# A two-pass rescaling kernel: the last stretch moved in 1 MB pieces in place of 2 MB ones

## What is computed

```python
x = x + _L0_conv_ref(_gn(x), w1, w2, g1, b1, g2, b2, lw1, lb1, lw2, lb2)
# _gn(v):        ((g - mean) / sqrt(var + eps)) in 32 groups
# _L0_conv_ref:  num = softmax(linear(linear(dot_cb)), axis=1);  return x * num[:, :, None, None]
```

## Time and profile before

| | us |
|---|---|
| median of 3 runs | 1735.64 |
| lowest, highest | 1733.91, 1736.18 |
| the profiled execution | 1736.04 |
| its span in the trace | 1734.3 |
| last stretch, from the first scaling of batch 1 to the end of the span | 587.9 |

### The profile page before, as it was taken

One profiled execution on the slowest core, in us unless ns is written; L12 is line 12 of the kernel. 1 busy time (PEld: TensorE's weight loads), 2 busy tenths in 40 slices (PEclk: granted clock), 3 DMA queues, 4 the chain that ended last, 5 costly groups with the idle time before them and its releaser, 6 DMA issues.

```text
span 1734.3 us, 12474 instructions
## 1 busy us (share of the span) xinstructions
PE 473.8 (27%) x3186; PEld 155.4 (9%) x3186; DVE 936.0 (54%) x4043; ACT 649.2 (37%) x504; POOL 327.8 (19%) x432
## 2 busy tenths in 40 slices
PE   3588756532223233233232332510000000000000
PEld 1233212110000010001000010100000000000000
DVE  5899999934655666555765557862222222222220
ACT  4688887853534545435454445400000000000000
POOL 7678888820000000000000000000000000000000
PEclk8799988866566665665666666755555555555555
DMA  9999999979999999999999998999999999999999
GB/s 390 426 426 426 404 413 426 428 295 425 425 432 429 429 431 429 431 431 429 430 431 429 430 425 348 372 384 433 429 430 433 430 431 433 430 431 433 430 431 394
DMA packets 52281, 725.97 MB, mean 419 GB/s; under 512 B 6257, under 2 KB 6769, under 8 KB 8050
## 3 DMA queue, kind: packets, MB, share of 16 engines
q1 hardware_dynamic: 34066, 460.94, 62.7%
q10 hardware_dynamic: 18144, 264.25, 35.8%
HBM read 456.73 MB, written 268.44 MB: 418 GB/s over the span
## 4 chain that ended last, share of the span: by engine, by line
DMA 54%; another core or an unknown queue 26%; DVE 6%; PE 4%; ACT 4%; issue 1%; SPq 1%; POOL 1%; ACTq 0%; POOLq 0%; DVEq 0%
DMA xs<-in_x 42%; DMA out<-xs 10%; DVE mul_junk L843 4%; PE ps_part L493 2%; ACT sq_junk L663 2%; DVE xs L920 2%; ACT xs L724 2%; DMA z<-in_w 1%; SPq L313 1%; PE ps_l L586 0%; PE ps_l L574 0%; SPq L260 0%; PE ps_y L594 0%; POOL rstd_b L401 0%
## 5 line engine op out<-in xcount | busy, mean ns | idle before, releaser
L843 DVE SCALAR_TENSOR_TENSOR mul_junk<-xs,ps_w 128x256 fp8e5<-128x256 f32 x1856 | 642.3, 415 | 275.0 <-DMA xs<-in_x 246.5
L663 ACT ACTIVATE sq_junk<-xs 128x4096 fp8e5<-128x4096 f32 x128 | 463.2, 3619 | 383.3 <-DMA xs<-in_x 363.2
L493 PE MATMUL ps_part<-xs,taps 128*32 128x512 f32 x2048 | 330.0, 800 | 619.7 <-DMA xs<-in_x 619.7
L920 DVE TENSOR_SCALAR xs<-xs,scale,shift 128x4096 f32<-128x4096 f32 x98 | 243.1, 2501 | 402.0 <-DMA xs<-in_x 401.4
L493 PEld LDWEIGHTS ps_part<-xs,taps 128*32 128x32 f32 x2048 | 88.5, 141 | 834.6 <-issue 815.3
L843 DVE DVE_READ_ACCUMULATOR mul_junk<-xs,ps_w 128x1 f32 x1856 | 151.2, 81 | 0.0
L401 POOL TENSOR_TENSOR rstd_b<-var,minus_half 128x2 f32<-128x2 f32 (+1 forms) x16 | 12.5, 778 | 689.3 <-DVE var L870 689.3
L373 POOL TENSOR_TENSOR prod<-xs,w_copy 128x768 f32<-128x768 f32 x64 | 116.6, 1828 | 60.3 <-DMA xs<-in_x 57.6
L724 ACT ACTIVATE xs<-xs,shift,scale 128x4096 f32<-128x4096 f32 x30 | 113.7, 3789 | 11.1 <-DVE xs L920 5.7
L379 POOL TENSOR_TENSOR prod<-prod 128x384 f32<-128x384 f32 x64 | 63.2, 1011 | 0.0
L383 POOL TENSOR_TENSOR prod<-prod 128x192 f32<-128x192 f32 x64 | 36.8, 600 | 0.0
(11 more groups left out here) (101 smaller groups left out, 280.6 us busy)
## 6 DMA issues: line engine op xcount, KB each, us to landing
xs<-in_x SPq DMA_DIRECT2D x215, 2048.0 KB, 25.0
out<-xs ACTq DMA_DIRECT2D x126, 2048.0 KB, 27.0
xs<-in_lw SPq DMA_DIRECT2D x2, 2048.0 KB, 21.3
out<-xs SPq DMA_DIRECT2D x2, 2048.0 KB, 11.0
w_c<-in_w_rows SPq DMA_DIRECT2D x1, 512.0 KB, 4.3
w_sb<-in_w SPq DMA_DIRECT2D x1, 512.0 KB, 9.5
z<-in_w SPq DMA_DIRECT2D x1, 512.0 KB, 23.6
affine_in<-in_g SPq DMA_DIRECT2D x2, 16.0 KB
```

Source lines behind the costliest of these rows:

```text
L493: last = nc.tensor.matmul(ps_part[g % 2][32 * a:32 * a + 32, :], taps[:, g % 2, hf * JH + j, :], xs[:, s[0]:s[1] + 1:s[1] - s[0], j * W:(j ...
L663: nc.scalar.activation(sq_junk[:], xs[:, s, :], ACT.Square, accum_out=sq_sum[:, u % 2, u // 2, b:b + 1], saturate=False).then_inc(squared, 1)
L843: last = nc.vector.scalar_tensor_tensor(out=mul_junk[:, sets[0] % 2, j - first, :], in0=xs[:, s, j * W:(j + 1) * W], scalar=1.0, saturate= ...
L920: return nc.vector.tensor_scalar(xs[:, s, :], xs[:, s, :], scale[:, b, g:g + 1], shift[:, b, g:g + 1], ALU.mult, ALU.add)
```

## The change

`CUTS` = 2 and `CUT` = `HALF // CUTS` (2048 elements) are new, and each half-unit of the last stretch is moved in two pieces of 128 x 2048, 1 MB, 8 KB in each partition. Each slot gets four semaphores of its own for it: `last_loaded[s][c]` and `last_stored[s][c]` for `c` = 0, 1; the last stretch no longer uses `x_loaded` and `x_stored`, except that loads 5 to 8 still wait for the batch 0 stores. SP issues 118 loads in place of 59, VectorE 128 scalings in place of 64, ScalarE's queue 128 stores in place of 64. A piece's load waits for the store of the same piece, nine half-units earlier. Nothing ahead of the last stretch is changed.

```diff
+CUTS = 2
+CUT = HALF // CUTS
+HELD_IN = (5, 4, 8, 6, 7)
...
-for _i in range(UNITS):
-    if _i >= HELD:
-        LOADS[last_slot(_i)].append(("last", _i))
-    STORES[last_slot(_i)].append(("last", _i))
...
+        last_loaded = [[sem(f"last_loaded{s}_{c}") for c in range(CUTS)] for s in range(S)]
+        last_stored = [[sem(f"last_stored{s}_{c}") for c in range(CUTS)] for s in range(S)]
...
+        def cut(u, c):
+            return slice((u % 2) * HALF + c * CUT, (u % 2) * HALF + (c + 1) * CUT)
...
             for i in range(HELD, UNITS):
                 s, u = last_slot(i), LAST_ORDER[i]
-                if i < S:
-                    sp.wait_ge(x_stored[s], written(s, ("x", UNITS - S + i, 0)))
-                else:
-                    sp.wait_ge(x_stored[s], written(s, ("last", i - S)))
-                sp.dma_start(xs[:, s, :], x_v[u // 2, :, 1, part_of(u)]).then_inc(x_loaded[s], 16)
+                for c in range(CUTS):
+                    if i < S:
+                        sp.wait_ge(x_stored[s], written(s, ("x", UNITS - S + i, 0)))
+                    else:
+                        sp.wait_ge(last_stored[s][c], 16 * (i // S))
+                    sp.dma_start(xs[:, s, cut(0, c)], x_v[u // 2, :, 1, cut(u, c)]).then_inc(last_loaded[s][c], 16)
             for s in range(S):
                 sp.wait_ge(x_stored[s], 16 * len(STORES[s]))
+                items = [i for i in range(UNITS) if last_slot(i) == s]
+                for c in range(CUTS):
+                    sp.wait_ge(last_stored[s][c], 16 * len(items))
...
             for i, u in enumerate(LAST_ORDER):
-                act.wait_ge(scaled_last, i + 1)
-                store(u, 1, last_slot(i))
+                s = last_slot(i)
+                for c in range(CUTS):
+                    act.wait_ge(scaled_last, CUTS * i + c + 1)
+                    act.dma_start(out_v[u // 2, :, 1, cut(u, c)], xs[:, s, cut(0, c)]).then_inc(last_stored[s][c], 16)
...
             for i, u in enumerate(LAST_ORDER):
                 s = last_slot(i)
-                if i >= HELD:
-                    dve.wait_ge(x_loaded[s], landed(s, ("last", i)))
-                scaled_by_dve(s, 1, u // 2).then_inc(scaled_last, 1)
+                g = u // 2
+                for c in range(CUTS):
+                    if i >= HELD:
+                        dve.wait_ge(last_loaded[s][c], 16 * (i // S if last_slot(i) in HELD_IN else i // S + 1))
+                    nc.vector.tensor_scalar(xs[:, s, cut(0, c)], xs[:, s, cut(0, c)], scale[:, 1, g:g + 1],
+                                            shift[:, 1, g:g + 1], ALU.mult, ALU.add).then_inc(scaled_last, 1)
```

## The result

The changed kernel takes 1741.16 us (median of 8 runs, 1739.4 to 1744.55), the kernel before 1736.3 us (8 runs beside them). The ratio on record is 1.0031 (the two medians alone give 1.0028), with a 95% interval of 1.0022 to 1.0040, or 3.8 to 6.9 us more. The forecast was 1741.4 us in a range of 1737.0 to 1749.0, with slower as the likely side.

A forecast was written before the change was run, and what follows sets the result against it. The prediction took the DMA engines' own time (bytes plus a cost per packet) to bound the last stretch. 1736.04 + 5.5 (packets) + 0.3 (last waits) + 0 = 1741.8, set to 1741.4 us against the median; range 1737.0 to 1749.0.

The forecast's parts named there:

- What bounds the stretch: Last stretch: the DMA engines' own time sets the period, 9.73 us per half-unit at 431 GB/s, not load or store delays.
- The packet term, 5.5 us: Last stretch: 1107 more packets on each engine at 5 ns beside their bytes, 5.5 us more.
- The 2 KB rows: Packet price from 2 KB loads set against 16 KB loads beside all engines' work: 6.6 ns per packet, 7.4 us.
- The 8 KB rows: Upper bound on packet price from a short window of 8 KB loads: 0.6 us per MB, 9.7 us over the stretch.
- The costless edits: Last stretch: VectorE's halved scalings and the added load and store issues fit inside existing waits and cost nothing.
- The 0.3 us for the last waits: Kernel's end: SP's 18 more waits, bounded by 0 and two issues of 0.33 us, taken as 0.3 us.
- Start and end, 0 us: Both ends of the last stretch: earlier first store and last scaling win nothing, 0 us; gain bounded by 1.2 + 1.5 us.
- The rival of a full queue: Last stretch: 14 queued stores block issues, perhaps holding up loads, 5 to 10 us beside the 5.5; with costs above 10, 0.08.
- A fixed cost for each DMA: Last stretch: rival named together with the full queue; the prediction said the trace disagrees as long as queues are deep.
- A cost in the loads or the stores alone: Last stretch: named as a sign that would make the forecast fall; no size given.
- The free pieces: Last stretch: smaller packets cost nothing and GB/s stays at 431; chance 0.11.
- the finer exchange: Last stretch: load and store packets alternate twice as often, 431 up to 437 GB/s, gain 8.1 us, 1727.6; chance 0.06.

The follow-up runs named there:

- e3: The change with four pieces in place of two (512 KB, 4 KB rows), against the kernel before: ratio 1.0090, +15.6 us.
- e1: Kernel before with 8 KB rows (alternate quarters of the group's row), still 2 MB DMAs; against the kernel before: ratio 1.0011, +1.9 us.
- e2: Kernel before with 1 MB DMAs split by odd and even partitions, still 16 KB rows; against the kernel before: ratio 1.0016, +2.8 us.
- e4: Kernel before with only VectorE's scalings in halves, loads and stores still 2 MB; against the kernel before: ratio 0.9997, -0.5 us.
- e8: The kernel before once more, nothing changed, as a kernel of its own; against the kernel before: ratio 0.9999, -0.2 us.
- e5: Kernel before with only the loads in two 1 MB pieces (8 KB rows), stores and scalings whole; against the kernel before: ratio 1.0034, +5.9 us.
- e12: Kernel before with only the loads' rows 8 KB, all DMAs 2 MB, output rows permuted; against the kernel before: ratio 1.0028, +4.9 us.
- e11: Kernel before with only the stores' rows 8 KB, all DMAs 2 MB, output rows permuted; against the kernel before: ratio 1.0013, +2.3 us.
- e10: Stores in two 1 MB pieces, loads still 2 MB DMAs but with 8 KB rows too; against the kernel before: ratio 1.0033, +5.7 us.
- e9: Loads in two 1 MB pieces, stores still 2 MB DMAs but with 8 KB rows too; against the kernel before: ratio 1.0022, +3.8 us.
- e6: Kernel before with only the stores in two 1 MB pieces, loads and scalings whole; against the kernel before: ratio 1.0088, +15.3 us.

## Why the prediction was right

- **What bounds the stretch.** Right, and shown: with every extra wait, issue and scaling of the change the share stayed at 1.01, and only the bytes per microsecond fell. The period was 9.81 us where 9.82 was said, and the rate 427 where 427 was.
- **The packet term, 5.5 us.** The price taken was 5 ns, in a span of 1.7 to 8.8. The stretch itself gives 4.4 ns (0.30 us per MB for 68.6 more packets per MB), which is 4.9 us over 1107 packets, and e3's three times as many give 4.7 ns. That a packet's cost and not a DMA's lowers the rate is shown by e1 and e2; that the totals follow from it holds within some 2 us, which the ends of e1 and e2 take up. The 2 KB rows at 42 us had said 6.6. The 8 KB rows had said more than the 8.8 that the prediction took from them, which carries their 0.6 us per MB over as it stands: by packets it is 0.63 us for 55.8 more per MB, 11.2 ns and 12.4 us, so the upper bound was worked out too low, from a window of 3 us. Against the 6.6, taking something off for loads that run beside busy engines was right in sign, and the size of what was taken off was a guess between two bounds that happened to lie well. A packet cost of 6.6 ns would have given 7.3 us, beyond the measured interval.
- **The costless edits.** VectorE's halves cost nothing (e4). The 0.3 us for the last waits is too small to be seen.
- **Start and end, 0 us.** The stretch began at 1148.57 us and not at 1146.41. The prediction named a shift of more than a microsecond as something that would speak against it. That was too strict: in e8, the kernel before, the stretch begins at 1144.67, and over the other traces, all with the same code ahead of it, at 1144.9 to 1148.7. The end was taken as the same; it differs by 1.2 us between traces with the same DMAs (losses of 3.7 us before and 2.5 in e4), and by 3.3 us between e1 and e2, which is what blurs their totals.
- **The rival of a full queue.** Its sign came: store issues of 4.26 us where more than 0.445 was to mean a full queue. Its price did not. ScalarE's queue has nothing else to do here, the loads' issues stayed at 0.328 us in the median, and while the queue blocked the engines' share stayed at 1.01. Where the loads' own queue blocks, in e5 and e12, what comes on top of 4.4 ns for each packet is 3.6 and 2.9 us, under the 5 to 10 that the prediction priced it at. A fixed cost for each DMA is not seen either: with 123 more of them e2 runs at 430 GB/s where 431 was.
- **A cost in the loads or the stores alone**, the prediction's other sign against itself, did not show: the rate fell with 8 KB rows in the stores only (e11, 37.24 us per MB) and with 8 KB rows in the loads only (e12, 37.32).
- **The free pieces and the finer exchange** fell with the rate, 427 and neither 431 nor 437. The range's lower end, 1737.0, is that of free pieces; no run shows a packet that costs nothing beside its bytes, and the runs with smaller packets show 4.2 to 4.7 ns. It is the size of the rows, 8 KB against 16, that e1 and e10 show to cost, at equal or larger DMAs. That loads and stores take turns, which the finer exchange starts from and e9's expectation too, is in the packet records. They don't name the engine, but the record of a packet on an engine begins 3 or 4 ns before that of the one ahead ends. Where only one packet fits so, from 1200 to 1680 us and the 4-byte packets left aside, the next is of the other queue in all of 5229 cases in the kernel before and in all of 16,496 in the change. In e5 a 16 KB store packet was followed by an 8 KB load packet in all 4138 cases, and a load packet by a store packet in 4128 and by another load packet in 3233. A turn is 309 ns in the change where it was 611, and nothing is won by it.

What stays open is e6: that unequal packets together with 1 MB stores cost 15 us is measured, and that single packets take up to more than twice as long as the rest is seen in its trace; why they do is not known. That its engines fall out of step is seen too, and not tied to a cause. Whether e2's long end comes from its DMAs, and the backlog at the loads in e9 and e1, are open as well.

## What to carry to other kernels

Where the DMA engines are the bound and their queues stay filled, as in this stretch, cutting transfers bought nothing (427 GB/s against 431): count the packets instead (a row of one partition each, and one for the semaphore on each engine), which took 4.2 to 4.7 ns of every engine's time here (e1, the change, e3), and look at the end, where 1 to 3 us hung on how evenly the engines finished. Before pieces are made smaller to hand over sooner, look whether anything waits for the hand-over that the bound resource doesn't hide. And cut loads and stores alike: where only the loads had the shorter rows (e5, e12) the backlog stood at the loads, 50.1 and 60.9 us to landing, and the last scaling and store stood bare at the end. With all rows of 8 KB but only the loads in two DMAs (e9) the backlog stood at the loads as well, 43.6 us.

## What was not expected of the hardware

- Cutting the stores alone cost nearly three times as much as cutting both: +15.3 us against +5.4. Cutting the loads alone cost as much as both, +5.9.
- With 16 KB stores beside 8 KB loads (e5), a load took 50 us to land and a store 11, in the medians, where with equal 16 KB rows a load took 18 and a store up to 68.
- An issue of a 1 MB store blocked for 4.26 us in the median with the 8 KB rows of the change. The number and the size of the DMAs don't explain it: e2's 1 MB stores with 16 KB rows took 0.54 us to issue, and e11's 2 MB stores with 8 KB rows 7.6 us in the median and up to 24, at +2.3 us in all (the lines below, e2 first). By an estimate from the median time to landing, the stores of the kernel before have some 62 packets waiting on each engine (66.8 / 9.73 x 9) and those of e2 some 64 (62.3 / 4.87 x 5), which don't block; those of the change have 91 (49.9 / 4.91 x 9) and those of e11 107 (61.5 / 9.75 x 17), which do. So it seems to begin at some 90 packets; e1's stores, with 91 (52.3 / 9.8 x 17), hardly block, 0.54 us in the median. No run tests the number of waiting packets by itself.
- e1's 2 MB loads in two runs a row took 0.54 us to issue and not 0.328.
- The last of the sixteen DMA engines goes on alone for 1 us (e8) or 2 (the kernel before) at the end of traces with the same DMAs, for 3 in e2, and for 5 to 6 in e6.

```profile
L807 ACTq DMA_DIRECT2D out<-xs x128: 478/539/1548, 1150.0 to 1706.2; - x128
...
L803 ACTq DMA_DIRECT2D out<-xs x58: 542/7600/23972, 1162.8 to 1699.2; - x58
```
